# All mask additions on GpSimd from step 19 on, with VectorE making the masks at the end of its step

## What is computed

```
h = jnp.maximum(_layernorm(x, axis=-1), 0.0)
neib_att = jnp.tanh(neigh @ Wn1 + bn1) @ Wn2 + bn2
value = neigh @ Wv + bv
x_att = jnp.tanh(h @ Wx1 + bx1) @ Wx2 + bx2
ws = jnp.einsum('nh,mh->nm', x_att, neib_att)
ws = jax.nn.leaky_relu(ws, negative_slope=0.01)
ws = jnp.where(adj > 0, ws, jnp.float32(NEG_BIG))
ws = jax.nn.softmax(ws, axis=1)
out = x + jnp.concatenate([h @ Wfx + bfx, ws @ value], axis=1)
```

## Time and profile before

| what | value |
|---|---|
| median of 3 runs | 548.64 us (547.9 to 549.05) |
| the profiled execution, its own time | 552.71 us |
| its span, first to last instruction | 550.5 us |
| mean granted TensorE clock over the span | 0.983 of full speed |
| busy share PE, DVE, ACT, POOL | 92%, 87%, 79%, 38% |

### The profile page before, as it was taken

How to read it: one execution, slowest core, us unless ns; L and a number is a source line. 1 busy time by engine, 2 the same in 40 slices (tenths; PEclk the granted TensorE clock), 3 DMA queues, 4 the chain that set the end, 5 groups by cost and what they waited for, 6 DMA issues and landing times.

```text
span 550.5 us, 8742 instructions
## 1 busy us (share of the span) xinstructions
PE 505.3 (92%) x2759; PEld 378.3 (69%) x2759; DVE 478.2 (87%) x883; ACT 432.7 (79%) x585; POOL 211.8 (38%) x325
## 2 busy tenths in 40 slices
PE   5798788899999999999999999999999999998996
PEld 4455556677777767766877677766777686776784
DVE  2669897999999999999999999999998999996664
ACT  2563688898888888888888878888888889897553
POOL 1402123234633654355434553456435444440100
PEclk8898999899999999999999999999999999999999
DMA  7752865454456545664356445643565445620100
GB/s 205 190 166 48 143 135 98 92 115 78 76 87 139 89 69 96 117 135 76 59 107 147 73 78 113 119 91 64 95 114 96 77 74 94 113 46 1 40 1 19
DMA packets 38013, 52.00 MB, mean 94 GB/s; under 512 B 3920, under 2 KB 29776, under 8 KB 37968
## 3 DMA queue, kind: packets, MB, share of 16 engines
q0 software_dynamic: 9216, 33.56, 37.5%
q1 hardware_dynamic: 28752, 17.90, 11.3%
HBM read 80.81 MB, written 4.19 MB: 154 GB/s over the span
## 4 chain that ended last, share of the span: by engine, by line
PE 34%; DVE 16%; issue 11%; ACT 11%; POOL 7%; DMA 3%; DVEq 1%; POOLq 0%; ACTq 0%
PE ps_turned L884 10%; POOL scores L421 6%; DVE pt_lo L655 5%; PE ps_scores L861 5%; PE ps_product L903 4%; PE ps_product L905 4%; PE ps_product L904 4%; ACT scores L512 4%; ACT scores L524 4%; DVE mask L642 4%; DVE scores L676 3%; PE ps_scores L860 3%; DMA adj_in<-in_adj 3%; ACT pt_hi L489 2%; PE ps_product L814 1%
## 5 line engine op out<-in xcount | busy, mean ns | idle before, releaser
L421 POOL TENSOR_TENSOR scores<-scores,mask 128x512 f32<-128x512 f32 x109 | 129.2, 1186 | 203.6 <-ACT scores L512 203.6
L655 DVE TENSOR_TENSOR pt_lo<-ps_turned,pt_hi 128x512 fp32r<-128x512 f32 x256 | 175.1, 685 | 32.1 <-ACT pt_hi L489 15.9
L489 ACT ACTIVATE pt_hi<-ps_turned 128x512 fp32r<-128x512 f32 x256 | 152.5, 597 | 55.6 <-PE ps_turned L884 49.5
L884 PE MATMUL ps_turned<-ident,scores 128*128 128x128 f32 x1024 | 158.3, 277 | 11.4 <-DVE pt_lo L655 11.0
L884 PEld LDWEIGHTS ps_turned<-ident,scores 128*128 128x128 f32 x1024 | 119.9, 141 | 61.3 <-DVE pt_lo L655 30.4
L512 ACT ACTIVATE scores<-ps_scores 128x1024 f32<-128x1024 f32 x128 | 131.1, 1025 | 28.7 <-PE ps_scores L861 25.9
L524 ACT ACTIVATE scores<-scores,neg_top 128x2048 f32<-128x2048 f32 x64 | 127.9, 1998 | 0.0
L676 DVE CUSTOM_DVE_ANT_0 scores<-ps_scores,scores,top 128x1024 f32<-128x1024 f32 x96 | 122.2, 1273 | 2.8 <-ACT scores L512 0.9
L903 PE MATMUL ps_product<-pt_hi,v_hi 128*128 128x512 f32 x256 | 113.1, 442 | 0.2 <-DVE pt_lo L655 0.2
L861 PE MATMUL ps_scores<-neib,xs 128*128 128x512 f32 x256 | 109.9, 507 | 0.0
L905 PE MATMUL ps_product<-pt_lo,v_hi 128*128 128x512 f32 x256 | 101.4, 396 | 0.0
(11 more groups left out here) (76 smaller groups left out, 385.1 us busy)
## 6 DMA issues: line engine op xcount, KB each, us to landing
adj_in<-in_adj POOLq DMA_DIRECT2D x64, 512.0 KB, 5.5
scores<-in_L_gnn_neigh SPq DMA_DIRECT2D x8, 512.0 KB, 4.3
x_rows<-in_x SPq DMA_DIRECT2D x8, 512.0 KB, 6.6
x_left<-in_x SPq DMA_DIRECT2D x8, 256.0 KB, 5.7
x_right<-in_x SPq DMA_DIRECT2D x8, 256.0 KB, 2.9
out_h<-x_left SPq DMA_DIRECT2D x8, 256.0 KB, 2.3
out_h<-x_right SPq DMA_DIRECT2D x8, 256.0 KB, 5.1
scores<-in_x SPq DMA_DIRECT2D x1, 512.0 KB, 5.0
```

Of the source, the lines that this page charges most:

```text
L421: pool.tensor_tensor(half, half, mask[:, s % 2, BANK:CHUNK], ALU.add).then_inc(masked, 1)
L489: act.activation(pt_hi[:, (2 * b + u) % HI_RING], pt[:, u], ACT.Copy).then_inc(hi_done, 1)
L655: dve.tensor_tensor(pt_lo[:, u], pt[:, u], pt_hi[:, (2 * b + u) % HI_RING].bitcast(FP32), ALU.subtract).then_inc(lo_done, 1)
L884: last = pe.transpose(pt[:, u, i * P:(i + 1) * P], scores[:, parity * TILES + i, n * P:(n + 1) * P], ident[:, :])
```

## The change

It touches steps 19 to 127 alone. TensorE's mask matmul goes there; GpSimd adds the mask of both halves, in two instructions of 128x512, each of which raises `masked`; it now waits for the mask too. VectorE makes the mask of s+1 behind its second `lo` instead of between the two, waits for `masked` and no longer for `scored` before it overwrites a mask buffer that GpSimd read, and waits for both adds before the leak. TensorE's score no longer waits for the mask.

```diff
@@ gpsimd, step
                     parity, tile, c = chunk_of(s)
-                    pool.wait_ge(risen, s + 1 + PERIOD * it)
-                    half = scores[:, parity * TILES + tile, c * CHUNK + BANK:(c + 1) * CHUNK]
-                    pool.tensor_tensor(half, half, mask[:, s % 2, BANK:CHUNK], ALU.add).then_inc(masked, 1)
+                    pool.wait_ge(risen, s + 1)
+                    pool.wait_ge(mask_done, s + 1)
+                    for h in range(2):
+                        half = scores[:, parity * TILES + tile, c * CHUNK + h * BANK:c * CHUNK + (h + 1) * BANK]
+                        pool.tensor_tensor(half, half, mask[:, s % 2, h * BANK:(h + 1) * BANK], ALU.add).then_inc(
+                            masked, 1)
@@ vector, mask_of
-                if n >= 2:
+                if n - 2 >= POOL_MASKS:
+                    dve.wait_ge(masked, 2 * (k - 1 - POOL_MASKS))
+                elif n >= 2:
                     dve.wait_ge(scored, k - 1)
-                if n - 2 >= POOL_MASKS:
-                    dve.wait_ge(masked, k - 1 - POOL_MASKS)
@@ vector, step
                     if n >= POOL_MASKS:
-                        dve.wait_ge(masked, k + 1 - POOL_MASKS)
+                        dve.wait_ge(masked, 2 * (k + 1 - POOL_MASKS))
                 lo(s, 0, it)
-                if POOL_MASKS <= s < STEPS - 1:
-                    mask_of(s + 1, it)
                 ...
                 lo(s, 1, it)
+                if POOL_MASKS <= s < STEPS - 1:
+                    mask_of(s + 1, it)
@@ tensor, score
                 if h == 0:
-                    pe.wait_ge(mask_done, k + 1)
+                    if s < POOL_MASKS:
+                        pe.wait_ge(mask_done, k + 1)
...
-                on_pool = h == 1 and s >= POOL_MASKS
+                on_pool = s >= POOL_MASKS
                 if not on_pool:
                     pe.matmul(ps[:, s % 2, half], ident_bf16[:, :], mask[:, s % 2, half], start=True, stop=False)
```

## The result

The changed kernel takes 556.26 us (median of 4 runs, 554.76 to 557.4), the kernel before 548.85 in the same runs: a ratio of 1.0119, 95% interval 1.0062 to 1.0175. (Ratios leave out an execution more than 1.5% above the fastest of its kernel; medians keep it.) It is slower by 7.4 us, where 16 were forecast. The direction was right, the size was less than half. Of the four times that the prediction worked out, 554, that of the first rival (the mask slips in between the two adds), lies nearest.

The account below looks back on a forecast made before the run. ScalarE's chain through the exponential was the bound, then the loop through both adds; 6.1 groups at +2.4 (+14.6) and the last four pairs (+1.1) made +16 on 548.6: 565 us, range 550 to 576.

Parts of the forecast that it names:

- the first rival: Waiting mask gets in between GpSimd's two adds, VectorE's small work hides under the second: 59.6 us a group, 554 us, chance 0.22.
- The bound, and the loop that takes over: ScalarE's chain gives way to relu, adds, leak, lo, turn, relu: at least 6.73 us a pair of steps against 6.46.
- The last leg: From TensorE's turn through the hi to the next relu: shrinks from 1.32 to 1.12 us without the mask matmul.
- The mask nearly always finds the second add begun or queued and waits until 3.39: VectorE's mask behind the second lo waits for both adds, ends 3.66 us after the relu, delaying leak and small work.
- window of 2.15 to 2.27: Time after the relu, in us, from the mask's earliest start to the first add's end, needed for slipping in.
- the pair of step 14: Two steps opened by step 14 mod 16: GpSimd comes late to its adds, `x_stack_low` follows; 8.1 us.
- The mask's place: Behind the second lo the mask stands directly ahead of the leak; between the two lo it held up neither.
- L860's 0.22 us: TensorE's stream time for the dropped mask matmul, taken off the turn-to-relu leg and the TensorE step, 2.94 to 2.72 us.
- the faster rival: The loop of adds does not end last; dropping the matmul saves at most 24 us, half giving nothing: 537, chance 0.10.
- the table of pairs: Times for the eight pairs of steps in a 16-step group, 6.9 to 8.3 us, sum 61.8 against 58.99; +2.4 taken.
- The signs of being wrong: Leak over 0.3 us after both adds in most steps, or the mask taking 0.41 us nearly everywhere.
- The clock: Pauses in TensorE's stream could lower its granted clock; new pauses are of the same kind, so no price or chance.

Follow-up runs that it names:

- The cut at 320: The changed kernel with GpSimd's two adds cut at column 320 instead of 512: 562.04 us, ratio 1.0244 to the kernel before.
- two pairs of kernels: Mask behind both lo against between them: loop 397.5 against 409.3 us with both adds, 371.4 against 380.3 with one add and no mask matmul.
- the cut at 704: The changed kernel with GpSimd's two adds cut at column 704 instead of 512: 559.65 us, ratio 1.0167 to the kernel before.
- one_add_of_1024: The changed kernel with one GpSimd add of 128x1024 in place of two of 128x512: 560.65 us, ratio 1.0182 to the kernel before.

## Why the prediction was off

- **The bound, and the loop that takes over:** right. Leg by leg the profile after has 3.39, 0.28, 1.87 where 3.39, 0.27 and 1.95 stood, and the turn's wait for the lo grew from 24 to 67 us. The last leg was too short: 1.55 us from the turn to the relu in the pair from step 124, not 1.12, since the hi waits there for the exponential. The forecast called 6.73 a floor, and one plain pair takes just that.
- **"The mask nearly always finds the second add begun or queued and waits until 3.39":** this step failed. In 32 of 109 pairs of adds the mask got in at the boundary, and VectorE's small work ran under the second add. The cut at 320, which takes that away, costs 6.1 us in the loop. The prediction had this as its first rival, with 0.22 and 554 us. Its window of 2.15 to 2.27 was right to 0.1 us, and its 59.6 us a group is what three groups of the changed kernel take. Two things were wrong. So narrow a window was thought to be seldom hit, but the same steps hit it in group after group. And the window was taken for the only way in: in the pair of step 14 the prediction itself has GpSimd late to its adds, which puts the boundary far behind the mask. That pair was put at 8.1 us and took 7.7; with the cut at 320 it took 8.6.
- **The mask's place:** it was put down as a harm, with "it held up neither" for the place before. It did hold up the second lo. The place is worth -8.9 to -11.8 us in the loop, shown by two pairs of kernels.
- **L860's 0.22 us:** it entered only through two legs of a pair. With TensorE's wait for the mask it is worth 10.4 us in the loop and 14 in the medians, about the price (half of 24) that the prediction gave it in the faster rival.
- **The second add:** never priced by itself. It costs 26 to 29 us in the loop, or 0.24 to 0.27 a step.
- **The sum:** +16 against +6.8 in the loop and +7.4 in the medians. Of the 9 us between, 6 are the slipped masks. The other 3 are in the table of pairs, which the kernel with the cut at 320 tests, since no mask slips in there. Its five groups from step 26 on cost 1.7 us more than before on average, not 2.4, while the first steps, put at nothing, cost 1.9. One of them, from relu 58 to 74, takes 61.7 us where the table sums to 61.8, but that is luck: its pairs lie up to 0.7 off on both sides (9.0 for 8.3 in 10, 8.6 for 8.1 in 14, 7.3 for 7.6 in 4, 7.0 for 7.3 in 12).
- **The signs of being wrong:** neither came. The leak starts more than 0.3 us after both adds in 54 of 109 steps, which is not most, and 37 masks of 108 take over 0.6 us. They could not have told the forecast from its first rival.
- **The clock:** as said, no part of it. It was 0.982 after and 0.983 before.

## What to carry to other kernels

A change with several parts can be the sum of large terms of both signs: here +26, -10 and -9. Price each by itself, from who waits behind whom, before adding up; kernels with one part each settle it. Where two engines exclude each other, ask what stands behind the instruction that will wait, and put the one that collides where only something that waits for the same release comes next, provided that its own readers have it early enough. And an instruction cut in two is a place for the other engine to get in, which can hide more than it costs.

## What the runs showed of the hardware

- A VectorE mask that had begun before the boundary of two GpSimd adds issued back to back got in between them: in all 32 such steps of the changed kernel, and in all 45 with the cut at 704. The pair of adds then took 2.46 to 2.53 us instead of 2.28. The Trainium skill ("SBUF — State Buffer", "Who interferes with whom") has the shared ports held for a whole instruction, the later one fully blocked. The rows agree: a mask of 8 columns takes 0.15 us at the least and 0.44 on average, and one of 1024 columns takes up to 1.77 (in one_add_of_1024). They show besides that the wait ends with the GpSimd instruction that is running, even when the next is queued behind it.
- GpSimd's time for the adds of a step is 2.28 us in two pieces of 512 or of 320 and 704, and 2.12 to 2.16 in one of 1024.
- The prologue, the same in all kernels, took 97.4 to 103.1 us up to the relu of step 19. A difference of 1% in one execution's span proves nothing here. The loop time is better, but late `adj` loads put about 3 us into one of them.
